# A Mamba layer with a top-2 mixture of experts: B and C of later chunks split on TensorE and ScalarE, eighteen drives by token instead of fourteen, and three steps of the routing moved

## The chip, the cores and the metric

The kernel runs on one core of a Trainium2 chip. The metric is the device time of one execution in microseconds (us), lower is better. A core has five engines with a queue each, and each works through its queue strictly in the order written: TensorE (PE, matrix products and transposes), VectorE (DVE), ScalarE (ACT), GpSimd (POOL) and SyncE (SP, which only issues DMAs). They wait for one another through semaphores.

## The reference, cut to what matters

```python
x_conv = silu(conv(x @ W_in[:, :256]));  z = x @ W_in[:, 256:]
Bm, Cm = split(x_conv @ W_x, 2)                       # 16 states each
dt = softplus(x_conv @ W_dt + b_dt)
h  = exp(dt * A_n) * h + (dt * u) * B_n               # over time, for each of 16 states n
y  = sum_n(h * C_n) + x_conv * D
x  = layernorm(x + (y * silu(z)) @ W_out)             # 2 x 1024 tokens, 128 wide
# then: top 2 of 8 experts by x @ w_g, capacity 640, gelu MLP 128 -> 512 -> 128,
# weighted sum back, residual, layernorm
```

## The kernel before, in words

The 2048 tokens are worked in four chunks (0 to 3) of 512 tokens, and each chunk in 16 units, one for each state: 64 units, numbered U = 0 to 63. U is in chunk U // 16 and has the place n = U % 16 there. The 256 channels lie as two halves d = 0, 1 of 128 partitions.

What a unit needs, and who makes it:

- **decay**, exp(dt * A_n): ScalarE, two 128x512 instructions into PSUM (`decays`, L1074).
- **drive**, dt * u * B_n. The usual way: TensorE spreads the row B_n over all partitions (`spread_b`, one matmul, L648), VectorE multiplies it with dtu (`drives`, one 128x1024 instruction, L1649), between the two scans of the unit before. The other way, for the units in the table `TURNED`: ScalarE makes it with tokens in partitions (`drive_by_token`, four 128x256 instructions, L1105, into the one buffer `drive_t`), and TensorE turns it back with two times four transposes (`turn_drive`, L664). Such a "turned" unit has no VectorE drive, and its decay is one 128x1024 instruction into `decay_sb` (L1069). The two PSUM banks of spread rows are also those of the turned drives, so the drive of the unit behind a turned one is made a unit earlier (`drive_beside`).
- **scan**: VectorE, two 128x512 scans (L1678), d = 0 and d = 1.
- **product** with C_n: GpSimd, one 128x1024 instruction (`multiply`, L1436). The states have a ring of 3 buffers, the products 4.
- **sum** into y: TensorE, `add_to_y`, eight 128x128 transposing matmuls (L678), in the last chunk four instructions of 512 columns (L673). It is queued two or more units behind (`SUMS`).

Around the units each engine's loop holds the rest of the layer, at a place n that tables or `if n ==` give: the projections of the next chunk (`bc_job`, `dt_job`, `conv_job`, `z_job` on TensorE, `take_...` and `soften_...` on ScalarE, `finish_dt` and `times_u` on GpSimd), and the end of the chunk before: `gate` on VectorE, then `start_y`, `turn_y` and `project_out` on TensorE, then the routing (`sort`, `mark`, `take_ranks`, `share`, `place_weights` on VectorE; `score`, `add_exps`, `weigh` on GpSimd) and 8 scatters of rows to the experts' slots, issued one per unit from GpSimd (`scatter`, L1517).

B and C of a chunk are kept to float32 precision as three bfloat16 parts in `bc_parts`. Chunk 0's parts are made on VectorE. For chunks 1 to 3 `take_bc` on ScalarE writes the leading part, and `split_bc` on GpSimd makes the rest with three 128x512 instructions (L1446, L1448, L1450), which two DMAs of SyncE's queue bring into place (`place_parts`).

`JOBS` lists the users of the two PSUM banks in which these side jobs pass (bank 0, 1; bank 2 for the last ranks), in order: a job waits until the one before it in its bank has been taken. `PAUSES` (units 30 and 61) are where ScalarE changes its table for silu.

Behind unit 63 come the routing of chunk 3, its scatters, and the experts: an MLP stage that TensorE fills.

## Time and profile before

| | |
|---|---|
| median of 3 runs | 385.12 us (383.41 to 385.39) |
| the profiled execution | 384.32 us, its span 382.6 us |
| busy in the span | PE 286.2 us, DVE 282.6 us, ACT 211.8 us, POOL 266.2 us |
| first scan to last | 24.91 to 255.1 us |
| first scan of chunk 1, 2, 3 | 79.51, 137.90, 196.87 us |

In rows of the timeline the columns are start, duration, engine, line, operation, output <- inputs, count and, in brackets, idle time before with the one who released it. Merged rows (x2 and more) give the time from the first's start to the last's end. DVE instructions overlap a little: a drive of 1.20 us is followed by the next instruction 1.11 to 1.12 us after its start. TensorE's rows likewise.

### The profile page before, as it was taken

How to read it: one execution, taken by the hardware profiler on the slowest of the kernel's cores; microseconds unless marked ns; L12 is line 12 of the kernel's file. 1: busy time of each engine (PE TensorE's matmuls, PEld its weight loads, DVE VectorE, ACT ScalarE, POOL GpSimd, SP SyncE). 2: the span in 40 equal slices, each digit the busy share in tenths (PEclk: the TensorE clock that was granted, in tenths of full speed). 3: DMA queues.
4: the chain of work that ended last, by engine and by line, in shares of the span. 5: the costliest groups of instructions: out<-in, count | busy, mean ns of one | idle time of the engine just before them, and what ended most of it. 6: DMA issues, size and time to landing. Idle time of an engine off the chain costs nothing. (4 is left out here: it accounts for less than half of the span.)

```text
span 382.6 us, 5173 instructions
## 1 busy us (share of the span) xinstructions
PE 286.2 (75%) x1566; PEld 207.6 (54%) x1566; DVE 282.6 (74%) x429; ACT 211.8 (55%) x425; POOL 266.2 (70%) x226
## 2 busy tenths in 40 slices
PE   8797889678866867786545899774289999998700
PEld 6445547456745544675433454332278888887600
DVE  2699889999999899999899889986021333334565
ACT  2858987969675684777737455744003323331305
POOL 4507689978888999999999876985710555556532
PEclk9999999999999868997885999899589999999965
DMA  7061079473354263232123211001152444222873
GB/s 233 6 224 55 2 240 286 135 194 127 89 168 137 82 199 117 69 100 82 55 73 122 74 64 55 3 15 42 43 155 79 118 126 125 82 82 76 240 204 110
DMA packets 35786, 42.90 MB, mean 112 GB/s; under 512 B 3862, under 2 KB 26331, under 8 KB 35760
## 3 DMA queue, kind: packets, MB, share of 16 engines
q1 hardware_dynamic: 32336, 37.38, 31.9%
q0 software_dynamic: 2304, 4.24, 3.4%
q10 hardware_dynamic: 1120, 0.97, 0.8%
q8 instruction: 12, 0.20, 0.2%
q14 instruction: 14, 0.11, 0.1%
HBM read 30.11 MB, written 12.79 MB: 112 GB/s over the span
## 5 line engine op out<-in xcount | busy, mean ns | idle before, releaser
L1436 POOL TENSOR_TENSOR product<-state,c_wide 128x1024 f32<-128x1024 f32 x64 | 149.9, 2347 | 37.1 <-DVE state L1678 27.5
L1074 ACT ACTIVATE psum<-dt,a_neg 128x512 f32<-128x512 f32 x96 | 65.0, 686 | 53.1 <-DVE state L1678 51.8
L678 PE MATMUL psum<-ident,product 128*128 128x128 f32 x384 | 56.1, 295 | 24.5 <-POOL product L1436 24.5
L678 PEld LDWEIGHTS psum<-ident,product 128*128 128x128 f32 x384 | 47.4, 152 | 35.0 <-POOL product L1436 32.1
L1678 DVE TENSOR_TENSOR_SCAN state<-psum,drive 128x512 f32<-128x512 f32 x52 | 62.0, 1212 | 2.5 <-ACT psum L1074 2.3
L1649 DVE TENSOR_TENSOR drive<-dtu,psum 128x1024 f32<-128x1024 f32 x50 | 60.0, 1199 | 4.6 <-PE psum L648 4.5
L1678 DVE TENSOR_TENSOR_SCAN state<-psum,carry,drive 128x512 f32<-128x512 f32 x48 | 60.0, 1269 | 0.2
L1563 POOL DMA_INDIRECT result_rows<-state,result_at x30 | 30.3, 1010 | 40.7 <-DVE state L1892 33.4
L1517 POOL DMA_INDIRECT slot_rows<-sent,scatter_at x32 | 32.9, 1028 | 10.7 <-issue 6.6
L912 PE MATMUL psum<-product,fc_sb 128*128 128x320 f32 x128 | 36.1, 435 | 1.1 <-DVE product L1860 1.1
L1857 DVE TENSOR_SCALAR tags<-c_wide 128x10 f32<-128x10 f32 x8 | 1.3, 164 | 43.4 <-PE psum L901 43.4
L1337 ACT ACTIVATE u<-psum 128x640 f32<-128x640 f32 x16 | 11.3, 704 | 38.6 <-PE psum L912 37.9
L673 PE MATMUL psum<-product,ident 128*128 128x512 f32 x60 | 29.4, 619 | 1.6 <-POOL product L1436 1.6
L912 PEld LDWEIGHTS psum<-product,fc_sb 128*128 128x128 f32 x128 | 22.8, 190 | 11.3 <-issue 2.7
L1337 ACT ACTIVATE z_tok<-psum 128x640 f32<-128x640 f32 x16 | 11.3, 704 | 27.6 <-PE psum L912 18.8
L664 PE MATMUL psum<-ident,drive_t 128*128 128x128 f32 x112 | 18.7, 296 | 8.6 <-DVE drive L1649 7.6
L723 PE MATMUL psum<-x_chan,w_conv 128*128 128x512 f32 x48 | 23.4, 614 | 1.6 <-ACT sent L1178 1.6
L1105 ACT ACTIVATE drive_t<-dtu_t,b_t 128x256 f32<-128x256 f32 x56 | 23.7, 494 | 1.0 <-PE psum L664 0.9
L664 PEld LDWEIGHTS psum<-ident,drive_t 128*128 128x128 f32 x112 | 14.4, 152 | 16.1 <-issue 14.3
L648 PE MATMUL psum<-bc_parts,selector 128*128 128x512 bf16 x50 | 20.0, 404 | 2.0 <-DVE state L1678 1.5
L1678 DVE TENSOR_TENSOR_SCAN state<-decay_sb,carry,psum 128x512 f32<-128x512 f32 x16 | 19.6, 1261 | 0.4 <-issue 0.4
L673 PEld LDWEIGHTS psum<-product,ident 128*128 128x128 f32 x60 | 11.5, 200 | 14.0 <-issue 10.7
(256 smaller groups left out, 527.1 us busy)
## 6 DMA issues: line engine op xcount, KB each, us to landing
c_wide<-c_rows SPq DMA_DIRECT2D x32, 512.0 KB
slot_rows<-blank SPq DMA_DIRECT2D x8, 325.0 KB, 4.6
c_wide<-slot_rows SPq DMA_DIRECT2D x8, 325.0 KB, 3.4
result_rows<-zeros SPq DMA_DIRECT2D x8, 256.0 KB, 5.1
late_rows<-zeros SPq DMA_DIRECT2D x8, 256.0 KB
fc_sb<-in_c_fc SPq DMA_DIRECT2D x8, 256.0 KB
proj_sb<-in_c_proj SPq DMA_DIRECT2D x8, 256.0 KB
c_wide<-result_rows SPq DMA_DIRECT2D x8, 256.0 KB, 5.5
```

The costliest lines, as they stand in the source:

```text
L664: last = nc.tensor.transpose(psum[:, turned_bank(U, d), j * P:(j + 1) * P], drive_t[:, j, d * P:(d + 1) * P], ident[:, :])
L673: nc.tensor.matmul(psum[:, Y_BANK + d, :], ident[:, :], product[:, i, d, :], start=False, stop=True, skip_group_check=True).then_inc(summe ...
L678: last = nc.tensor.matmul(y_part(j, d), product[:, i, d, j * P:(j + 1) * P], ident[:, :], is_transpose=True, start=False, stop=True, skip_ ...
L723: last = nc.tensor.matmul(psum[:, bank, :], w_conv[:, k, d * P:(d + 1) * P], x_of(q, k), start=(k == 0), stop=(k == D_CONV - 1))
L912: last = nc.tensor.matmul(psum[:, 2 + 2 * (h % 2) + s, 0:HALF], fc_sb[:, i, h * P:(h + 1) * P], rows_chan[:, i, s * HALF:(s + 1) * HALF], ...
L1074: nc.scalar.activation(psum[:, A_BANK + d, :], dt[:, q % 2, d, :], ACT.Exp, scale=a_neg[:, n:n + 1]).then_inc(decay_ready, 1)
L1105: nc.scalar.activation(drive_t[:, j, :], dtu_t[:, j, :], ACT.Copy, scale=b_t[:, q % 2, j, n:n + 1]).then_inc(drive_t_ready, 1)
L1436: nc.gpsimd.tensor_tensor(product[:, U % PRODUCTS, channels, :], state[:, U % RING, channels, :], wide, ALU.mult).then_inc(product_ready, 1)
L1517: gp.indirect_dma_start(out=slot_rows, out_offset=bass.IndirectOffsetOnAxis(ap=scatter_at[:, k, j:j + 1], axis=0), in_=sent[:, k, j, :], i ...
L1563: gp.indirect_dma_start(out=result_rows, out_offset=bass.IndirectOffsetOnAxis(ap=result_at[:, i, s:s + 1], axis=0), in_=rows_out[:, i, s, ...
L1649: nc.vector.tensor_tensor(drive[:, drive_number(U) % 2, :, :], dtu[:, q % 2, :, :], psum[:, b_bank(U), :].unsqueeze(1).to_broadcast([P, DT ...
L1678: nc.vector.tensor_tensor_scan(state[:, U % RING, d, :], decay, rows, before, ALU.mult, ALU.add).then_inc(scanned, 1)
```

## The change

Five things are changed together.

1. `TURNED` has 18 units instead of 14: chunk 1 has 19, 21, 23, 26, 28, 31 (was 19, 22, 26, 29), chunk 2 has 43, 45, 47 (was 43, 46), chunk 3 has 51, 53, 55, 57, 60 (was 51, 54, 57, 60). There are two buffers for them: `drive_t` and, from its last use on, `conv_rows_sb`. Turned units may now stand two apart; the second one's first half then waits for the first one's second scan.
2. For chunks 2 and 3 the middle and low parts of B and C are made by TensorE and ScalarE: `rest_job` adds minus the part just cast to the same PSUM bank (one bfloat16 matmul of 512 columns), `take_rest` casts what is left, twice. `split_bc` and `place_parts` stay for chunk 1 alone.
3. `dt_job`, `take_dt_job`, `soften_...`, `finish_dt` and `times_u` of the next chunk stand at other places n, `JOBS` has another order, and `center_w_out` with `take_w_cat` moves one unit ahead.
4. `share` (the reciprocal) moves from behind unit SHARE[q] to between the two scans of the unit after it.
5. The scatters of chunk 1's rows move from n = 14, 15 of chunk 2 and n = 0 to 5 of chunk 3 to n = 4 to 11 of chunk 3.

```diff
-TURNED = (4, 7, 10, 14, 19, 22, 26, 29, 43, 46, 51, 54, 57, 60)
+TURNED = (4, 7, 10, 14, 19, 21, 23, 26, 28, 31, 43, 45, 47, 51, 53, 55, 57, 60)
...
-        drive_t = sb("drive_t", [P, TPC, D_INNER])
+        drive_t = [sb("drive_t", [P, TPC, D_INNER]), conv_rows_sb]
...
             def turn_drive(U, d):
                 pe.wait_ge(drive_t_ready, TPC * (TURNED.index(U) + 1))
                 pe.wait_ge(drive_ready, drive_number(U) + d)
+                if d == 0 and U - 2 in TURNED:
+                    pe.wait_ge(scanned, DT * (U - 1))
...
+            def rest_job(q, part):
+                bank, _ = JOB[f"bc{q}"]
+                pe.wait_ge(minus_eye_made, 1)
+                if part == 0:
+                    pe.wait_ge(bc_cast, q - 1)
+                else:
+                    pe.wait_ge(bc_parted, q - 1)
+                rows = slice(64 * part, P)
+                nc.tensor.matmul(psum[:, W_BANKS[bank], :], minus_eye[rows, :], bc_parts[rows, q * CH:(q + 1) * CH], start=False, stop=True,
+                                 skip_group_check=True).then_inc(bc_rest_made, 1)
...
                     if n == q - 1 and q < NQ - 1:
                         bc_job(q + 1)
-                    elif n in (q, 2 * q) and q < NQ - 1:
-                        dt_job(q + 1, n // q - 1)
+                    if q < NQ - 1 and n in (q + 1, q + 2):
+                        rest_job(q + 1, n - q - 1)
+                    if q < NQ - 1 and n in (1, 3):
+                        dt_job(q + 1, n // 2)
+                    if q == 2 and n == 4:
+                        dtu_job(2, 0)
...
+            def take_rest(q, part):
+                bank, _ = JOB[f"bc{q}"]
+                act.wait_ge(bc_rest_made, 2 * (q - 2) + part + 1)
+                lanes = slice(64 + 32 * part, P)
+                nc.scalar.activation(bc_parts[lanes, q * CH:(q + 1) * CH], psum[lanes, W_BANKS[bank], :], ACT.Copy).then_inc(w_taken[bank] if part else bc_parted, 1)
...
-                    if n >= PLACE[q] and U < LAST - 1:
+                    if n >= PLACE[q] and q != 2 and U < LAST - 1:
                         scatter_some(q - 1, n - PLACE[q], 1)
-                    if q >= 2 and n < RUNS // NQ - EARLY[q - 1]:
-                        scatter_some(q - 2, n + EARLY[q - 1], 1)
+                    if q == 2 and n < RUNS // NQ - EARLY:
+                        scatter_some(0, n + EARLY, 1)
+
+                    if q == 3 and PLACE[q] - RUNS // NQ <= n < PLACE[q]:
+                        scatter_some(1, n - PLACE[q] + RUNS // NQ, 1)
...
                 scan(U, 0)
                 if drive_beside(U):
                     drives(drive_beside(U))
+                if q and n == SHARE[q] + 1:
+                    share(q - 1)
                 scan(U, 1)
...
-                    if n == SHARE[q]:
-                        share(q - 1)
```

The first place is TensorE at units 18 to 20, the start of chunk 1. L578 (L584 in the changed kernel) with `w_dt_sb` is a `dt_job`, L664 (L677) a `turn_drive`, L632 (L638) is `start_y`, L678 (L691) `add_to_y`, L648 (L658) `spread_b`. Before:

```order
L578 MATMUL psum<-u,w_dt_sb 128x512 x2
L664 MATMUL psum<-ident,drive_t 128x128 x4
L578 MATMUL psum<-u,w_dt_sb 128x512 x2
L664 MATMUL psum<-ident,drive_t 128x128 x4
L632 MATMUL psum<-diag_d,u 128x128 x8
L678 MATMUL psum<-ident,product 128x128 x16
L648 MATMUL psum<-bc_parts,selector 128x512
```

and in the changed kernel, with L727 the new `rest_job`:

```order
L584 MATMUL psum<-u,w_dt_sb 128x512 x2
L677 MATMUL psum<-ident,drive_t 128x128 x4
L727 MATMUL psum<-bc_parts,minus_eye 128x512
L677 MATMUL psum<-ident,drive_t 128x128 x4
L638 MATMUL psum<-diag_d,u 128x128 x8
L691 MATMUL psum<-ident,product 128x128 x16
L727 MATMUL psum<-bc_parts,minus_eye 128x512
L584 MATMUL psum<-u,w_dt_sb 128x512 x2
```

The second `dt_job` of the chunk has moved from ahead of the first unit's sums to behind them, together with a `rest_job`, and both stand ahead of the spread that follows.

The second place is ScalarE at units 34 to 36 of chunk 2. L1074 (L1103) are decays, L1082 (L1111) a copy of the last state, L1021 and L1022 (L1050, L1051) are the two halves of a `take_dt_job`. Before:

```order
L1117 ACTIVATE bc_sb<-psum 128x512
L1118 ACTIVATE bc_parts<-psum 128x512
L1074 ACTIVATE psum<-dt,a_neg 128x512 x2
L1082 ACTIVATE carry<-state 128x2
L1021 ACTIVATE soft<-psum,channel_sb 128x512
L1022 ACTIVATE dt<-psum,channel_sb 128x512
L1074 ACTIVATE psum<-dt,a_neg 128x512 x2
L1082 ACTIVATE carry<-state 128x2
L1021 ACTIVATE soft<-psum,channel_sb 128x512
L1022 ACTIVATE dt<-psum,channel_sb 128x512
```

and in the changed kernel, with L1157 the new `take_rest`:

```order
L1149 ACTIVATE bc_sb<-psum 128x512
L1150 ACTIVATE bc_parts<-psum 128x512
L1050 ACTIVATE soft<-psum,channel_sb 128x512
L1051 ACTIVATE dt<-psum,channel_sb 128x512
L1103 ACTIVATE psum<-dt,a_neg 128x512 x2
L1111 ACTIVATE carry<-state 128x2
L1157 ACTIVATE bc_parts<-psum 64x512
L1050 ACTIVATE soft<-psum,channel_sb 128x512
L1051 ACTIVATE dt<-psum,channel_sb 128x512
L1103 ACTIVATE psum<-dt,a_neg 128x512 x2
```

Both halves of dt are taken one unit sooner, and a `take_rest` stands ahead of the second. TensorE's queue there has its `start_y`, the sum of unit 32, the spread for unit 37, the `rest_job` and then the `dt_job` that this take waits for.

The third place is GpSimd in chunk 3, units 51 to 57, with L1436 (L1478) the product and L1517 (L1557) a scatter. Before:

```order
L1436 TENSOR_TENSOR product<-state,c_wide 128x1024
L1517 DMA slot_rows<-sent,scatter_at 5120x130
L1436 TENSOR_TENSOR product<-state,c_wide 128x1024
L1517 DMA slot_rows<-sent,scatter_at 5120x130
L1436 TENSOR_TENSOR product<-state,c_wide 128x1024
L1517 DMA slot_rows<-sent,scatter_at 5120x130
L1436 TENSOR_TENSOR product<-state,c_wide 128x1024 x4
L1477 TENSOR_SCALAR half_var<-sum_squares 128x4
```

and in the changed kernel:

```order
L1557 DMA slot_rows<-sent,scatter_at 5120x130
L1478 TENSOR_TENSOR product<-state,c_wide 128x1024
L1557 DMA slot_rows<-sent,scatter_at 5120x130
L1478 TENSOR_TENSOR product<-state,c_wide 128x1024
L1557 DMA slot_rows<-sent,scatter_at 5120x130
L1478 TENSOR_TENSOR product<-state,c_wide 128x1024
L1557 DMA slot_rows<-sent,scatter_at 5120x130
L1478 TENSOR_TENSOR product<-state,c_wide 128x1024
L1517 TENSOR_SCALAR half_var<-sum_squares 128x4
```

The scatters of the first units are gone (seven products stand together ahead of this piece), and the products of units 54 to 56, which stood together, now have a scatter between them. The same holds for units 57 to 59: `score`, `add_exps` and `weigh` each have a scatter behind them in the changed kernel.

## Rows read from the trace of the kernel before

**Rows 1.** The page's head.

```profile
span 382.6 us, 5173 instructions
```

**Rows 2.** Busy by stretch: start:end, length, PE, PEld, DVE, ACT, POOL, PE clock, DMA, GB/s.

```profile
198.00:255.00 57.00, 44.87 (x152) 24.15 (x152) 54.17 (x70) 35.46 (x70) 48.36 (x38) 0.85 0.17 57
...
150.40:153.80 3.40, 3.40 (x18) 3.40 (x17) 3.40 (x4) 1.62 (x4) 2.93 (x3) 0.50 0.26 84
```

**Rows 3.** The page's groups: busy, mean ns of one, idle before and its releaser.

```profile
L1436 POOL TENSOR_TENSOR product<-state,c_wide 128x1024 f32<-128x1024 f32 x64 | 149.9, 2347 | 37.1 <-DVE state L1678 27.5
L1074 ACT ACTIVATE psum<-dt,a_neg 128x512 f32<-128x512 f32 x96 | 65.0, 686 | 53.1 <-DVE state L1678 51.8
...
L1649 DVE TENSOR_TENSOR drive<-dtu,psum 128x1024 f32<-128x1024 f32 x50 | 60.0, 1199 | 4.6 <-PE psum L648 4.5
...
L1105 ACT ACTIVATE drive_t<-dtu_t,b_t 128x256 f32<-128x256 f32 x56 | 23.7, 494 | 1.0 <-PE psum L664 0.9
```

**Rows 4.** ScalarE's groups: a decay in one piece.

```profile
L1069 ACT ACTIVATE decay_sb<-dt,a_neg 128x1024 f32<-128x1024 f32 x14 | 15.9, 1136 | 0.0
```

**Rows 5.** VectorE's timeline: gate and drive in chunk 1, reciprocals, last weights.

```profile
89.95 1.19 DVE L1685 TENSOR_TENSOR z_tok<-z_tok,psum 128x1024 f32<-128x1024 f32 x1
...
95.58 1.22 DVE L1649 TENSOR_TENSOR drive<-dtu,psum 128x1024 f32<-128x1024 f32 x1 [0.89 <-PE psum L648]
...
128.26 0.18 DVE L1766 RECIPROCAL denom<-denom 128x4 f32<-128x4 f32 x1 [1.23 <-POOL denom L1497]
...
190.84 0.18 DVE L1766 RECIPROCAL denom<-denom 128x4 f32<-128x4 f32 x1 [1.58 <-POOL denom L1497]
...
245.26 0.17 DVE L1808 TENSOR_TENSOR sent<-weight,psum 128x8 f32<-128x8 f32 x1
```

**Rows 6.** TensorE's timeline behind the gate of chunk 1.

```profile
91.63 1.95 PE L632 MATMUL psum<-diag_d,u 128*128 128x128 f32 x16
93.41 1.91 PE L678 MATMUL psum<-ident,product 128*128 128x128 f32 x16
95.16 0.38 PE L648 MATMUL psum<-bc_parts,selector 128*128 128x512 bf16 x1
```

**Rows 7.** TensorE's timeline, chunk 3: output projection to a turned drive.

```profile
218.50 0.70 PE L770 MATMUL psum<-w_cat,y_chan 128*128 128x136 f32 x4 [1.23 <-ACT y_chan L1169]
...
219.96 0.60 PE L664 MATMUL psum<-ident,drive_t 128*128 128x128 f32 x4
```

**Rows 8.** TensorE's timeline behind the gate of chunk 2.

```profile
149.52 3.00 PE L632 MATMUL psum<-diag_d,u 128*128 128x128 f32 x16 [2.40 <-DVE z_tok L1685]
...
153.92 0.38 PE L648 MATMUL psum<-bc_parts,selector 128*128 128x512 bf16 x1
...
155.23 1.88 PE L578 MATMUL psum<-u,w_dt_sb 128*128 128x512 f32 x4
```

**Rows 9.** VectorE's timeline, second scan of unit 36.

```profile
155.48 1.22 DVE L1678 TENSOR_TENSOR_SCAN state<-psum,drive 128x512 f32<-128x512 f32 x1
```

**Rows 10.** GpSimd's timeline: a scatter; units 42, 46's weights; units 52, 55, 56, 57; weights.

```profile
144.53 1.01 POOL L1517 DMA_INDIRECT slot_rows<-sent,scatter_at  x1 [0.17 <-issue]
...
178.20 2.35 POOL L1436 TENSOR_TENSOR product<-state,c_wide 128x1024 f32<-128x1024 f32 x1 [0.93 <-issue]
...
193.07 0.21 POOL L1501 TENSOR_TENSOR weight<-exps,denom 128x8 f32<-128x8 f32 x1
...
215.78 2.36 POOL L1436 TENSOR_TENSOR product<-state,c_wide 128x1024 f32<-128x1024 f32 x1 [0.79 <-DVE state L1678]
...
226.47 2.37 POOL L1436 TENSOR_TENSOR product<-state,c_wide 128x1024 f32<-128x1024 f32 x1 [1.20 <-PE psum L673]
231.16 2.37 POOL L1436 TENSOR_TENSOR product<-state,c_wide 128x1024 f32<-128x1024 f32 x1 [2.32 <-DVE state L1678]
234.64 2.36 POOL L1436 TENSOR_TENSOR product<-state,c_wide 128x1024 f32<-128x1024 f32 x1 [1.11 <-issue]
...
245.02 0.20 POOL L1501 TENSOR_TENSOR weight<-exps,denom 128x8 f32<-128x8 f32 x1
```

More of the change, by code:

```diff
@@ L475, in _ @@
                     store_c(m // (D_STATE // C_PAIR) + 1)
-                if m % (D_STATE // C_PAIR) == 6 and m // (D_STATE // C_PAIR) < NQ - 1:
-                    place_parts(m // (D_STATE // C_PAIR) + 1)
+                if m == 6:
+                    place_parts(1)
                 if m == C_SLOTS - 1:
@@ L637, in spread_b @@
                 if n == 0 and q:
-                    pe.wait_ge(bc_taken, 32 * q)
+                    if q == 1:
+                        pe.wait_ge(bc_taken, 32)
+                    else:
+                        bank, before = JOB[f"bc{q}"]
+                        pe.wait_ge(w_taken[bank], before + 1)
                 if U >= 2:
@@ L847, in _ @@
                     turn_drive(U + 1, 0)
-                if q == 2 and n in (6, 7):
-                    dtu_job(2, n - 6)
+                if q == 2 and n == 7:
+                    dtu_job(2, 1)
                 if q == 2 and n in (12, 14):
@@ L1095, in drive_by_token @@
                 q, n = divmod(U, D_STATE)
-                before = TURNED.index(U)
-                act.wait_ge(drive_turned, DT * before)
+                i = TURNED.index(U)
+                if i == 1:
+                    act.wait_ge(w_conv_made, 1)
+                if i >= 2:
+                    act.wait_ge(drive_turned, DT * (i - 1))
                 act.wait_ge(b_t_ready, q + 1)
@@ L1250, in _ @@
                         drive_by_token(T)
-                if q == 2 and n in (6, 7):
-                    take_dtu(2, n - 6)
+                if q == 2 and n in (4, 7):
+                    take_dtu(2, n // 7)
                 if q == 2 and n in (13, 15):
@@ L1267, in _ @@
                         take_bc(q + 1)
-                    elif n == first + 1:
+                    if q and n in (first + 1, first + 2):
+                        take_rest(q + 1, n - first - 1)
+                    if n == (first + 1, 2, 2)[q]:
                         take_dt_job(q + 1, 0)
-                    elif n == first + 2:
+                    elif n == (first + 2, 3, 3)[q]:
                         take_dt_job(q + 1, 1)
-                    elif n == first + 3:
+                    elif n == (first + 3, 4, 5)[q]:
                         soften_exp(q + 1)
-                    elif n == (first + 4 if q == 0 else first + 5):
+                    elif n == first + (5 if q == 2 else 4):
                         soften_log(q + 1)
@@ L1297, in _ @@
                         take_dtu(1, n - 14)
+                    if n == 15:
+                        take_w_cat()
                 else:
@@ L1318, in _ @@
                         copy_sent(q - 1)
-                    if q == 1 and n == 0:
-                        take_w_cat()
                     if q == NQ - 1 and n == 10:
@@ L1523, in scatter_some @@
                     scatter(i // TPC, TPC * q + i % TPC)
-            EARLY = [D_STATE - n for n in PLACE]
+            EARLY = D_STATE - PLACE[1]
             U_PLACE = (NQ - 1) * D_STATE + PLACE[NQ - 1]
```

39 lines of the change are left out of this document (22 added, 17 removed).

## The prediction

> **What bounds the kernel now.** I read the page's head and busy shares first, then busy time by stretch, then VectorE's timeline through all 64 units, and beside it those of GpSimd, TensorE and ScalarE wherever VectorE stood idle. The profiled execution took 384.3 us around a span of 382.6 [rows 1]; the median of the runs shown is 385.1, 0.8 above it. VectorE sets the pace of the units: in chunk 3 it is busy 54.2 of 57.0 us [rows 2], and a unit costs it two scans of about 1.2 and a drive of 1.2 [rows 3]. But GpSimd is close behind: 48.4 of the same 57.0 us, and the reader should see that its slack is not spread evenly. In chunk 2, from the product of unit 42 at 178.20 to the weights at 193.07, it works without a break [rows 10], and the reciprocal that waits 1.58 us is waiting for it [rows 5]. TensorE and ScalarE have time in sum, but their queues are in order, and a side job ahead of a spread or a decay delays VectorE.
>
> **Part 1, the four drives.** Each drive that leaves VectorE saves 1.12 us, since the next instruction starts that long after a drive of 1.20 [rows 3]. Two leave in chunk 1, one in chunk 2, one in chunk 3: 4.5 us. ScalarE takes four 128x256 instructions for each, 23.7 / 14 = 1.7 us [rows 3], and gives back two decays of 0.69 for one of 1.14 [rows 3, 4]: 1.5 us net, 6 us in all, into 53.1 us of its waiting for scans [rows 3]. As a sum that is hidden; place by place it is not, below.
>
> **Part 2, the split.** It frees GpSimd of three instructions in chunks 1 and 2, early in the chunk, where it waits for scans anyway: by itself nothing. On TensorE the two matmuls of a chunk cost like a spread, 0.4 us each [rows 6].
>
> **Part 3, what the moved jobs do in chunk 1.** The spread that unit 20's drive waits for starts at 95.16, behind `start_y` and two sums, and VectorE already idles 0.89 us there [rows 5, 6]. Now a rest matmul and a dt job stand between: next start 0.2 and 1.8 later, as the job's four matmuls take 1.88 [rows 8]. The same dt job leaves the place ahead of `start_y`, which can begin at the gate's end, 91.1 instead of 91.63 [rows 5, 6]: 0.4 back. So the drive comes 1.6 us late (bounds 0 and 2.3: full cover, and no 0.4 back). ScalarE takes that dt (two instructions of about 0.7) only from 97.0 on, and has queued behind it a drive by token (1.7), a softplus step, two decays, the whole decay of unit 23, a softplus step and two copies of y, about 1.0, 1.3, 1.1, 1.0 and 1.0, with pieces of 128x1024 at up to 1.14 [rows 3, 4]: y is copied at about 105.1. The output projection waits for it and stands ahead of the second half of turned unit 23. From such a projection's start to the end of the transposes was 219.96 + 0.60 - 218.50 = 2.1 us in chunk 3 [rows 7], and here 0.4 of B's transposes come on top: 107.6. VectorE would want it at 97.2 + 1.1 (drive) + 1.2 (scan) + 2.4 (unit 21) + 3.5 (unit 22) + 1.2 = 106.5. Cost 1.1 (0 to 2). At unit 23 the run is 1.6 + 1.1 late and one drive ahead, 1.6 behind before.
>
> The rest of chunk 1 pays: a second drive (1.1), and the reciprocal. It waited 1.23 us [rows 5] for sums that stood behind GpSimd's `times_u`; that is two units earlier now, and the reciprocal 2.3 later. The weights need GpSimd's next product to end, which leaves about 1.1 of the 1.23. Chunk 1: +1.6 - 1.1 - 1.1 = -0.6.
>
> **Chunk 2.** ScalarE must have the decay of unit 37 ready when unit 36's second scan ends, 155.48 + 1.12 = 156.6 [rows 9]. Its queue now holds, ahead of that decay, the take of a dt job that TensorE starts behind the spread of 153.92 and a rest matmul, at 154.35, and ends at 156.2 [rows 8]. Take 1.25, decay 0.65: 158.05. VectorE waits 1.4 us (0 to 1.5). TensorE is late partly because its granted clock was 0.50, the 1.2 GHz level, from 150.4 to 153.8 [rows 2]: `start_y` took 3.00 where it took 1.95 in chunk 1 [rows 6, 8]. I take the stretch as it was.
>
> The extra turned unit, 47, saves 1.1. The reciprocal saves nothing here. GpSimd's chain from the product of unit 42 to the weights is the same 193.07 - 178.20 = 14.9 us [rows 10]: five products, `times_u`, `score` and `add_exps`, none of them moved against unit 42. `place_weights` stands on VectorE behind the second scan of unit 46 and ends where it did. The 1.58 us just pass from the reciprocal to the weights. Chunk 2: +1.4 - 1.1 = +0.3.
>
> **Chunk 3.** The two scatters at the end of chunk 2 and six at the start of chunk 3 go to where VectorE is to become fastest. A scatter holds GpSimd 1.01 + 0.17, with the next start 1.2 later [rows 10]. Ahead of the weights that `place_weights` needs, counted from the product of unit 52, there were two scatters and there are now seven: 5 x 1.23 = 6.1 us. GpSimd's idle time there was 1.20 + 2.32 + 1.11 = 4.6 [rows 10]; it fills that, less about 0.3 in which it still waits for unit 57. So the weights come 6.1 - 4.6 + 0.3 = 1.8 later, and with them VectorE, which wrote them at 245.26 [rows 5], at once behind GpSimd's 245.02 [rows 10]. The fifth turned unit of the chunk saves VectorE 1.1, which it waits away at the weights. Chunk 3: +1.8 (bounds -2.3, if GpSimd keeps up and two TensorE waits between units 54 and 55 also go, and +3). Behind unit 63 the queues are the same, and the experts simply start as much later.
>
> **The sum:** -0.6 + 0.3 + 1.8 = +1.5, from the execution's own 384.3: 385.8. In the terms of the median 0.8 is added, 386.6; I give 386.2, between the two. A measurement of this kernel tells about 0.5%, 1.9 us, from no change, so my forecast reads as no difference, on the slow side.
>
> The trace shows TensorE at the lower level behind the gate of chunk 2 after it had been idle 2.4 us [rows 8]. The Trainium skill (TensorE: Matmul & The Clock Gate, section "What's actually happening") says the clock follows how busy TensorE has lately been, and the change gives it more work. By that rule the 1.4 us of chunk 2 would go. It would be 384.8 instead of 386.2; the trace agrees with the rule in that the level fell after idling.
>
> **Rivals.**
>
> - *VectorE alone bounds, and all cover holds.* 4.5 saved by drives and 1.23 + 1.58 by reciprocals [rows 5]: 7.3 off, 377.0 to 377.8. For it speaks VectorE's 95% in chunk 3 [rows 2]; against it GpSimd's unbroken 14.9 us, which no edit shortens.
> - *GpSimd keeps up in chunk 3.* If the weights don't wait, chunk 3 gives -2.3 instead of +1.8: 382.1. For it: GpSimd idles 4.6 us there and starts the chunk free of lag. Against it: 6.1 is more than 4.6.
> - *TensorE at its lower level behind the gate of chunk 1* (the slower side). There `start_y`, sums, spread, dt job, transposes and the projection now follow one another on the path. Sized by `start_y`, 3.00 against 1.95, a factor of 1.5 on 1.8 + 1.8 + 2.0 + 2.5 = 8 us: +4.1, and 390.3. It decides once the level falls between 91 and 106. For it: it fell behind chunk 2's gate [rows 2]. Against it: chunk 1's `start_y` ran fast [rows 6], and TensorE has more to do there now.
> - *TensorE at its full level behind the gate of chunk 2*: `start_y` 1.05 and the sum faster, so that the dt is taken in time; -1.4, and 384.8.
>
> **How the numbers follow.** Forecast 0.46; all cover holds 0.08; GpSimd keeps up 0.17; lower level in chunk 1 0.13; full level in chunk 2 0.16. The forecast's own range is 384.4 to 388.2, by its bounds of about 1 us each way on three terms. With no more than 2 in 10 left out, the range reaches down past the second rival and most of the way to the third: 381.6 to 389.4. Faster by over 0.5% means under 383.2: the first two rivals and a little of the others, 0.28. Slower by over 0.5% means above 387.1: the third rival and a third of the forecast's cases, 0.29. Within 0.5%: 0.43.
>
> **What would show it.** In the changed profile: VectorE's drive for unit 22 (its first behind unit 19) waits 2 to 3 us for a spread, not 0.89; the second scan of unit 23 waits about 1 us; the first scan of unit 37 waits over 1 us for a decay on ScalarE; the reciprocal waits under 0.3 us in chunk 1, and in chunk 2 the write of weights waits about 1.2; in chunk 3 GpSimd shows no gap from unit 52's product to the weights except about 0.3, and VectorE waits over 2 us in reciprocal and weights together. The forecast is wrong if the scatters hold GpSimd under 1 us each, if the weights are ready when VectorE comes to them, or if the drives' gains are still there at the first scan of chunk 2 and again at that of chunk 3.

## The result, and the profile after

The changed kernel takes 388.53 us in the median (386.78 to 389.56, 6 runs); the kernel before, on the same chip, 385.19 (383.41 to 385.44, 6 runs). The ratio is 1.0101 with an interval of 1.0077 to 1.0125: slower by 3 to 5 us. The prediction said 386.2 within 381.6 to 389.4. The time lies in the range, but 2.3 us above the figure and just above the 384.4 to 388.2 that the forecast allowed its own case. "No difference, on the slow side" had 0.43 of the chances and "slower by over 0.5%" 0.29; it is the second that was measured.

The page of the changed kernel, its head and two groups (busy us, mean ns | idle before and its releaser):

```profile
span 386.8 us, 5258 instructions
...
L1721 DVE TENSOR_TENSOR_SCAN state<-psum,drive 128x512 f32<-128x512 f32 x50 | 59.7, 1213 | 4.9 <-ACT psum L1103 4.7
L1692 DVE TENSOR_TENSOR drive<-dtu,psum 128x1024 f32<-128x1024 f32 x46 | 55.2, 1201 | 8.3 <-PE psum L658 8.2
```

VectorE does 46 drives, 55.2 us, where it did 50 in 60.0 [rows 3]. But the idle time in front of them rose from 4.6 to 8.3 us, behind TensorE's spreads, and that in front of this group of scans, behind ScalarE's decays, from 2.5 to 4.9. So the work was removed as planned, and the wait took its place.

The same in time. The columns are the stretch, its length, busy us and instructions of each engine, TensorE's granted clock and the DMAs. Each stretch goes from the first scan of a chunk to that of the next, the last one from the last scan to the end. First the kernel before:

```profile
79.51:137.90 58.39, 43.04 (x263) 31.38 (x262) 55.96 (x73) 42.25 (x82) 49.42 (x36) 0.96 0.44 139
137.90:196.87 58.97, 41.37 (x253) 32.60 (x251) 56.50 (x75) 39.78 (x88) 55.11 (x42) 0.87 0.29 95
196.87:255.05 58.18, 45.21 (x155) 24.15 (x152) 55.35 (x71) 36.42 (x72) 49.50 (x39) 0.85 0.17 57
255.05:382.60 127.55, 91.10 (x579) 76.20 (x579) 50.60 (x152) 34.78 (x78) 59.58 (x58) 0.88 0.38 111
```

and the changed kernel:

```profile
79.48:140.02 60.54, 45.76 (x272) 33.34 (x270) 53.81 (x71) 45.27 (x89) 45.61 (x32) 0.94 0.44 128
140.02:198.48 58.46, 41.82 (x253) 33.53 (x254) 55.51 (x74) 43.44 (x95) 52.34 (x39) 0.85 0.32 99
198.48:259.43 60.95, 46.80 (x171) 24.56 (x169) 54.26 (x70) 37.06 (x74) 49.48 (x39) 0.89 0.17 56
259.43:386.80 127.37, 90.82 (x579) 75.77 (x579) 51.56 (x151) 34.75 (x78) 60.31 (x58) 0.88 0.39 111
```

Chunk 1 is 2.15 us longer (60.54 against 58.39), chunk 2 0.51 shorter, chunk 3 2.77 longer, the experts 0.18 shorter: 4.2 us in the span. VectorE's busy time fell by 2.15, 0.99 and 1.09 us, which is what was bought.

Its waits, from VectorE's timeline of the changed kernel (start, duration, what it is, idle time before it and the releaser):

```profile
99.67 1.22 DVE L1692 TENSOR_TENSOR drive<-dtu,psum 128x1024 f32<-128x1024 f32 x1 [5.00 <-PE psum L658]
110.35 1.28 DVE L1721 TENSOR_TENSOR_SCAN state<-decay_sb,carry,psum 128x512 f32<-128x512 f32 x1 [1.26 <-issue]
...
144.18 1.22 DVE L1721 TENSOR_TENSOR_SCAN state<-psum,drive 128x512 f32<-128x512 f32 x1 [0.72 <-ACT psum L1103]
...
159.17 1.22 DVE L1721 TENSOR_TENSOR_SCAN state<-psum,drive 128x512 f32<-128x512 f32 x1 [0.31 <-ACT psum L1103]
184.89 1.22 DVE L1721 TENSOR_TENSOR_SCAN state<-psum,drive 128x512 f32<-128x512 f32 x1 [0.88 <-ACT psum L1103]
192.38 1.22 DVE L1721 TENSOR_TENSOR_SCAN state<-psum,drive 128x512 f32<-128x512 f32 x1 [0.68 <-ACT psum L1103]
...
215.74 1.22 DVE L1692 TENSOR_TENSOR drive<-dtu,psum 128x1024 f32<-128x1024 f32 x1 [2.09 <-PE psum L658]
245.67 0.18 DVE L1809 RECIPROCAL denom<-denom 128x4 f32<-128x4 f32 x1 [0.76 <-POOL denom L1537]
249.83 0.17 DVE L1851 TENSOR_TENSOR sent<-weight,psum 128x8 f32<-128x8 f32 x1 [2.70 <-POOL weight L1541]
```

The first row answers to the drive that waited 0.89 us [rows 5]: it now waits 5.00. The reciprocals of chunks 1 and 2, which waited 1.23 and 1.58, wait no more; that of chunk 3 and the write of weights wait 3.5 us together, where the write came at once behind GpSimd. The second row, 1.26 us, is the second scan of unit 23.

Behind the first row stands TensorE, in the changed kernel, from ahead of the gate to the spread:

```profile
85.92 0.60 PE L677 MATMUL psum<-ident,drive_t 128*128 128x128 f32 x4
89.43 0.58 PE L727 MATMUL psum<-bc_parts,minus_eye 128*128 128x512 bf16 x1 [2.91 <-ACT bc_parts L1150]
...
91.18 3.78 PE L638 MATMUL psum<-diag_d,u 128*128 128x128 f32 x16 [0.30 <-DVE z_tok L1728]
94.75 2.44 PE L691 MATMUL psum<-ident,product 128*128 128x128 f32 x16
97.12 0.39 PE L727 MATMUL psum<-bc_parts,minus_eye 64*128 64x512 bf16 x1
97.44 1.98 PE L584 MATMUL psum<-u,w_dt_sb 128*128 128x512 f32 x4
99.26 0.38 PE L658 MATMUL psum<-bc_parts,selector 128*128 128x512 bf16 x1
```

In the kernel before, two dt jobs stood there, with a shorter idle time ahead of each:

```profile
85.82 1.98 PE L578 MATMUL psum<-u,w_dt_sb 128*128 128x512 f32 x4 [1.71 <-ACT w_cat L1229]
...
89.37 1.98 PE L578 MATMUL psum<-u,w_dt_sb 128*128 128x512 f32 x4 [1.13 <-ACT bc_parts L1118]
```

TensorE's granted clock there (the column behind the bracket), in the changed kernel:

```profile
88.00:90.00 2.00, 0.57 (x2) 0.75 0.00 0
90.00:92.00 2.00, 1.70 (x9) 0.50 0.92 258
...
96.00:98.00 2.00, 2.00 (x14) 1.00 0.48 127
```

and in the kernel before:

```profile
90.00:92.00 2.00, 2.00 (x12) 1.00 0.90 262
```

`start_y` took 3.78 where it took 1.95, and the sums 2.44 where they took 1.91 [rows 6]: the clock was at its 1.2 GHz level (0.50), and back at the full one by 96 us. Of the 4.1 us that the wait grew, 1.83 + 0.53 is clock, less the 0.45 by which `start_y` began sooner, and 0.32 + 1.82 are the rest matmul and the dt job ahead of the spread (next start minus start).

In chunk 3 it is GpSimd, here from unit 52 to the weights:

```profile
218.29 2.34 POOL L1478 TENSOR_TENSOR product<-state,c_wide 128x1024 f32<-128x1024 f32 x1 [3.33 <-DVE state L1721]
...
236.20 2.36 POOL L1478 TENSOR_TENSOR product<-state,c_wide 128x1024 f32<-128x1024 f32 x1
...
241.44 1.09 POOL L1557 DMA_INDIRECT slot_rows<-sent,scatter_at  x1 [0.32 <-DVE state L1721]
...
246.23 1.04 POOL L1557 DMA_INDIRECT slot_rows<-sent,scatter_at  x1 [0.59 <-PE psum L686]
...
249.60 0.20 POOL L1541 TENSOR_TENSOR weight<-exps,denom 128x8 f32<-128x8 f32 x1
```

From the product of unit 52 to that of 57 no gap is left: five times product and scatter, (236.20 - 218.29) / 5 = 3.6 us each, while VectorE needs 3.5 for a unit with a drive and 2.4 for a turned one. From unit 52's product to the weights it takes 249.60 - 218.29 = 31.3 us, where it took 245.02 - 215.78 = 29.2 [rows 10].

The other part of chunk 3 lies ahead of unit 52: its product starts 218.29 - 198.48 = 19.8 us after the chunk's first scan, and it was 215.78 - 196.87 = 18.9. VectorE waited 2.09 us for the spread there where it had waited 1.17. This is the clock again. `start_y` has another form in this chunk, four matmuls; before and after:

```profile
210.32 2.64 PE L625 MATMUL psum<-u,diag_d 128*128 128x512 f32 x4
```
```profile
211.93 3.56 PE L631 MATMUL psum<-u,diag_d 128*128 128x512 f32 x4
```

It took 0.92 us longer, and the wait behind it is 0.92 longer. The gate was passed at the lower level in both kernels, but in the kernel before the granted clock was 1.00 from 212 us, and in the changed one still 0.50 up to 214 and 0.68 up to 216.

### The profile page after: what moved, and what is told of

It reads as the page before. It is cut to its first block and busy times, and to the rows that moved or that the text cites. A ratio compares the mean times of both kernels' runs of the same rounds, so it can differ in the third digit from the quotient of the medians.

```text
span 386.8 us, 5258 instructions
## 1 busy us (share of the span) xinstructions
PE 291.2 (75%) x1598; PEld 211.0 (55%) x1598; DVE 279.3 (72%) x425; ACT 219.1 (57%) x441; POOL 260.5 (67%) x221
## 5 line engine op out<-in xcount | busy, mean ns | idle before, releaser
L1478 POOL TENSOR_TENSOR product<-state,c_wide 128x1024 f32<-128x1024 f32 x64 | 149.9, 2347 | 47.4 <-DVE state L1721 38.9
L1103 ACT ACTIVATE psum<-dt,a_neg 128x512 f32<-128x512 f32 x88 | 59.0, 684 | 34.4 <-DVE state L1721 33.2
L691 PE MATMUL psum<-ident,product 128*128 128x128 f32 x384 | 54.1, 288 | 14.2 <-POOL product L1478 13.9
L1721 DVE TENSOR_TENSOR_SCAN state<-psum,drive 128x512 f32<-128x512 f32 x50 | 59.7, 1213 | 4.9 <-ACT psum L1103 4.7
L1692 DVE TENSOR_TENSOR drive<-dtu,psum 128x1024 f32<-128x1024 f32 x46 | 55.2, 1201 | 8.3 <-PE psum L658 8.2
L691 PEld LDWEIGHTS psum<-ident,product 128*128 128x128 f32 x384 | 46.2, 149 | 24.2 <-POOL product L1478 20.1
L1721 DVE TENSOR_TENSOR_SCAN state<-psum,carry,drive 128x512 f32<-128x512 f32 x42 | 52.8, 1271 | 0.4 <-ACT psum L1103 0.2
L1557 POOL DMA_INDIRECT slot_rows<-sent,scatter_at x32 | 32.8, 1025 | 10.4 <-issue 6.5
L1721 DVE TENSOR_TENSOR_SCAN state<-decay_sb,carry,psum 128x512 f32<-128x512 f32 x22 | 27.1, 1263 | 2.1 <-issue 1.7
L1098 ACT ACTIVATE decay_sb<-dt,a_neg 128x1024 f32<-128x1024 f32 x18 | 20.5, 1139 | 7.7 <-DVE state L1721 7.7
L658 PE MATMUL psum<-bc_parts,selector 128*128 128x512 bf16 x46 | 17.7, 389 | 3.7 <-DVE state L1721 2.9
L1721 DVE TENSOR_TENSOR_SCAN state<-decay_sb,psum 128x512 f32<-128x512 f32 x14 | 16.5, 1204 | 1.0 <-issue 1.0
L677 PE MATMUL psum<-ident,conv_rows_sb 128*128 128x128 f32 x72 | 11.5, 284 | 7.3 <-ACT drive_t L1137 2.8
```

The source lines that it names most:

```text
L691: last = nc.tensor.matmul(y_part(j, d), product[:, i, d, j * P:(j + 1) * P], ident[:, :], is_transpose=True, start=False, stop=True, skip_ ...
L1103: nc.scalar.activation(psum[:, A_BANK + d, :], dt[:, q % 2, d, :], ACT.Exp, scale=a_neg[:, n:n + 1]).then_inc(decay_ready, 1)
L1478: nc.gpsimd.tensor_tensor(product[:, U % PRODUCTS, channels, :], state[:, U % RING, channels, :], wide, ALU.mult).then_inc(product_ready, 1)
L1557: gp.indirect_dma_start(out=slot_rows, out_offset=bass.IndirectOffsetOnAxis(ap=scatter_at[:, k, j:j + 1], axis=0), in_=sent[:, k, j, :], i ...
L1692: nc.vector.tensor_tensor(drive[:, drive_number(U) % 2, :, :], dtu[:, q % 2, :, :], psum[:, b_bank(U), :].unsqueeze(1).to_broadcast([P, DT ...
L1721: nc.vector.tensor_tensor_scan(state[:, U % RING, d, :], decay, rows, before, ALU.mult, ALU.add).then_inc(scanned, 1)
```

## The experiments

My theory after this reading: four separate things happened. Scatters late in chunk 3 hold GpSimd; a dt job stands ahead of the spread behind chunk 1's gate; an idle TensorE lets the clock fall there; and what the drives and the reciprocal give is taken in part by GpSimd's chain. The rival is that the turned units overload ScalarE and the rest is noise around them. In the table medians are in us; the last column has the lengths of the chunks in us, from VectorE's timeline of one profiled execution each, cut at the first scan of each chunk as above (before 58.4, 59.0, 58.2; changed kernel 60.5, 58.5, 61.0). A chunk's length can differ by 1 us between two executions of the same instructions: up to unit 45 f2 has those of the kernel before, and its chunk 2 is already 0.9 us longer by then (59.9 in all, for 59.0). Line numbers in the rows below are those of the kernel they are from.

| kernel | median | before, same chip | ratio [interval] | chunk 1, 2, 3 |
|---|---|---|---|---|
| e1 turned alone | 384.21 | 385.85 | 0.9963 [0.9947, 0.9979] | 57.7, 59.9, 57.4 |
| e2 reciprocal alone | 385.56 | 385.85 | 0.9999 [0.9981, 1.0017] | 58.4, 59.0, 58.3 |
| e3 old scatters | 384.93 | 385.85 | 0.9985 [0.9969, 1.0002] | 60.6, 58.5, 57.6 |
| e4 split alone | 392.91 | 385.85 | 1.0157 [1.0121, 1.0193] | 63.1, 58.9, 59.1 |
| f1 fill idle | 384.29 | 385.30 | 0.9969 [0.9946, 0.9992] | 58.3, 58.5, 58.1 |
| f2 late scatters alone | 388.10 | 385.30 | 1.0063 [1.0043, 1.0083] | 58.5, 59.9, 61.6 |
| f3 weights later | 383.13 | 385.30 | 0.9938 [0.9907, 0.9968] | 56.6, 61.3, 58.1 |
| f4 dt behind spread | 385.07 | 385.30 | 0.9988 [0.9958, 1.0018] | 59.7, 58.4, 58.1 |
| g1 both orders | 383.41 | 385.62 | 0.9952 [0.9933, 0.9971] | 57.7, 58.3, 57.5 |
| g2 sixteen turned | 382.59 | 385.62 | 0.9935 [0.9910, 0.9960] | 57.7, 57.7, 57.4 |
| g3 weights of chunk 2 later | 383.90 | 385.62 | 0.9962 [0.9944, 0.9980] | 58.5, 58.6, 59.1 |
| h1 both and sixteen | 385.52 | 385.34 | 1.0005 [0.9987, 1.0023] | 60.2, 59.3, 58.3 |

**e1, the turned units alone.**

```diff
-TURNED = (4, 7, 10, 14, 19, 22, 26, 29, 43, 46, 51, 54, 57, 60)
+TURNED = (4, 7, 10, 14, 19, 21, 23, 26, 28, 31, 43, 45, 47, 51, 53, 55, 57, 60)
+drive_t in two buffers, with the waits that go with them
```

> The kernel before with one part of the change alone: the eighteen turned units (and the second buffer that they need). B and C are still split on GpSimd, no job is moved. My theory: the drives themselves are worth about 1.1 us each, 4 x 1.1 = 4.5 us less, so about 380.7 where before has 385.2; the loss of the whole change comes from the jobs and scatters that were moved. Rival: ScalarE's queue has no room, decays come late in chunks 1 and 2 as they do after the change, and half or more of it is given back: 383 to 385.

1.4 us less (0.37%), not 4.5: a third of what four drives are worth. VectorE's timeline of this kernel says who took the rest:

```profile
126.97 0.18 DVE L1771 RECIPROCAL denom<-denom 128x4 f32<-128x4 f32 x1 [2.34 <-POOL denom L1502]
140.79 1.22 DVE L1683 TENSOR_TENSOR_SCAN state<-psum,drive 128x512 f32<-128x512 f32 x1 [0.80 <-ACT psum L1076]
```

In chunk 1 one of the two drives went into the reciprocal, 2.34 us for 1.23 [rows 5]. In chunk 2 two decays of ScalarE came late (0.80 where 0.19 was waited before, and 0.89), and another 0.7 us of waits stands at 164 to 166; the chunk became 0.9 us longer. So the rival is right for chunk 2, GpSimd's chain for chunk 1.

**e2, the reciprocal alone.**

```diff
                     drives(drive_beside(U))
+                if q and n == SHARE[q] + 1:
+                    share(q - 1)
                 scan(U, 1)
...
-                    if n == SHARE[q]:
-                        share(q - 1)
```

> The kernel before with only the reciprocal moved behind the first scan of the next unit. My theory: its wait of 1.23 us in chunk 1 goes (1.1 kept), the 1.58 us of chunk 2 pass on to the write of weights: 1.1 less, 384.1 where before has 385.2. Rival: both waits go, 2.8 less, 382.4. Another rival: the write of weights takes over the wait in both chunks, no change, 385.2.

Nothing, with an interval of 0.7 us each way: the last rival. In chunk 1 the reciprocal has no wait left, and the write of weights has it:

```profile
130.64 0.17 DVE L1808 TENSOR_TENSOR sent<-weight,psum 128x8 f32<-128x8 f32 x1 [1.00 <-POOL weight L1501]
```

**e3, the old scatters in the changed kernel.**

```diff
-                    if n >= PLACE[q] and q != 2 and U < LAST - 1:
+                    if n >= PLACE[q] and U < LAST - 1:
...
-                    if q == 3 and PLACE[q] - RUNS // NQ <= n < PLACE[q]:
-                        scatter_some(1, n - PLACE[q] + RUNS // NQ, 1)
+                    if q >= 2 and n < RUNS // NQ - EARLY[q - 1]:
+                        scatter_some(q - 2, n + EARLY[q - 1], 1)
```

> The changed kernel with the scatters of chunk 1 back in their old places (two at the end of chunk 2, six at the start of chunk 3). My theory: five scatters fewer stand ahead of the weights in chunk 3, the 2.7 us wait of VectorE there goes: 2 to 2.8 us less, about 386.1 where the changed kernel has 388.5. Rival: the scatters then delay the products at the start of chunk 3 and give the same back: within 0.5 us of 388.5.

The ratio to before goes from 1.0101 to 0.9985: without the late scatters the change as a whole gains and loses nothing that can be measured. Chunk 3 is 57.6 us instead of 61.0, 3.4 less, more than I had from the wait at the weights alone (2.70), since the reciprocal's 0.76 goes too.

**e4, the split alone**: the changed kernel with these taken back, so that the split stays, with its job table and moved jobs.

```diff
-TURNED = (4, 7, 10, 14, 19, 21, 23, 26, 28, 31, 43, 45, 47, 51, 53, 55, 57, 60)
+TURNED = (4, 7, 10, 14, 19, 22, 26, 29, 43, 46, 51, 54, 57, 60)
-                if q and n == SHARE[q] + 1:
-                    share(q - 1)
+                    if n == SHARE[q]:
+                        share(q - 1)
+and the scatters as in e3
```

> The kernel before with the split of B and C by TensorE and ScalarE alone, and with it the dt jobs and the other jobs that it moves; turned units, reciprocal and scatters as before. My theory: TensorE is late with the spread behind the gate of chunk 1 (3 to 5 us wait instead of 0.9) and ScalarE with decays in chunks 1 and 2: 3 to 5 us more, about 389 where before has 385.2. Rival: the split only frees GpSimd and its jobs hide, within 1 us of 385.2; then the turned units are what overloads ScalarE.

The dearest part by its ratio: 1.6%, some 6 us, though its six executions spread from 389.3 to 394.6. Its first drive behind the gate waits 5.04 us, as after the whole change, and 4.7 of the 5.6 us that its last scan ends late lie in chunk 1. The profiled execution is the slowest of the six, and 4.5 us of its excess lie behind the last scan (132.0 us for 127.6), where the granted clock was 0.67 from 290.7 to 300.7 and the kernel before had 1.00 as far behind its last scan. Only the part up to the last scan is traced to the edit; how much of the 6 us the rest makes in the other executions stays open.

**f1, TensorE's idle time filled** (on e3).

```diff
+                    if q == 1 and n == 2:
+                        dt_job(2, 0)
                     if q < NQ - 1 and n in (q + 1, q + 2):
                         rest_job(q + 1, n - q - 1)
-                    if q < NQ - 1 and n in (1, 3):
+                    if q < NQ - 1 and n in (1, 3) and (q, n) != (1, 1):
                         dt_job(q + 1, n // 2)
```

> The changed kernel with the old places of the scatters, and with the first dt job of chunk 1 one unit later, ahead of the first rest matmul, where TensorE stood idle 2.9 us before its granted clock fell to 0.50. Its output is taken no sooner than it was, so nothing on the path moves. Theory of the clock: the level falls because of the idle time; with 1.0 us of it left the level stays at 1.00 from 90 to 96 us, `start_y` takes 1.95 and the two sums 1.9 (3.78 and 2.44 in the changed kernel), and the wait of VectorE's first drive behind the gate falls from 5.0 to about 2.6 us: 383 where the kernel with old scatters has 384.9. Rival, the order alone: the level falls all the same or makes no difference, and the wait stays at 5 us; 384.9.

The wait fell to 2.77 us, chunk 1 by 2.2 us. On TensorE, and its clock from 90 to 91 us:

```profile
89.79 0.38 PE L727 MATMUL psum<-bc_parts,minus_eye 128*128 128x512 bf16 x1 [1.55 <-ACT bc_parts L1152]
...
91.53 2.05 PE L638 MATMUL psum<-diag_d,u 128*128 128x128 f32 x16 [0.92 <-DVE z_tok L1727]
93.42 1.91 PE L691 MATMUL psum<-ident,product 128*128 128x128 f32 x16
```
```profile
90.00:91.00 1.00, 0.61 (x5) 1.00 0.54 193
```

The dt job is the same work on the same engine, 2 us later, and the level did not fall. This is one execution; the four that were profiled with the 2.91 us of idle time (changed kernel, e3, e4, f4) all had `start_y` at 3.78 or 3.79. 2.77 is near what the prediction's own sum gives (0.89 + 1.6 = 2.5). The whole time gained less, 384.3 for 384.9, and the intervals of the two ratios overlap: waits of 2.24 (for 2.10) and 0.8 us came in chunk 3, which is 0.6 us longer.

**f2, the late scatters alone** (on the kernel before, the lines of e3 the other way round).

> The kernel before with only the scatters of chunk 1 moved to just ahead of the weights of chunk 3. Theory of the prediction: GpSimd has 4.6 us idle there against 6.1 us of scatters, so 1.5 to 1.8 us more: 387.3 where before has 385.6. Theory of the first runs: the five scatters cost their full 3.4 us, as between the changed kernel and the one with old scatters: 389. Rival: nothing below 0.5 us, since VectorE is slower here than in the changed kernel and GpSimd keeps up: 385.6.

2.8 us more, between the two theories; chunk 3 alone is 3.4 us longer (61.6 for 58.2), 0.4 of it at the gate's spread (1.60 for 1.17), which leaves 2.9, in waits of 1.65 at the reciprocal and 1.54 at the weights. The prediction had 1.8 for it. The gaps that I took as filled are not: GpSimd still idles 1.04 us ahead of unit 56's product at 232.24, and 0.31 and 0.59 ahead of the scatters behind `score` and `add_exps`, 1.9 us and not 0.3.

**f3, the weights a unit later** (on the kernel before, with eighteen turned units and the reciprocal moved).

```diff
-        PLACE = [0, 13, 14, 12]
+        PLACE = [0, 14, 15, 12]
```

> The kernel before with the eighteen turned units, the reciprocal moved, and the write of weights and all that waits for it one unit later in chunks 1 and 2. Theory: GpSimd's chain up to the weights took in the drives' gains (VectorE's wait at the reciprocal rose to 2.34 and 1.72 us with the turned units alone); one unit later it is hidden, and both waits fall under 0.3: 3 to 4 us less than the turned units alone, 380.5 to 381.5 where before has 385.6. Rival: GpSimd is the bound over the whole chunk, the wait comes back at another place, and the time stays near 384.

383.1, and not 381: GpSimd's waits went, chunk 1 is the shortest of all (56.6), and then ScalarE is late. VectorE's timeline:

```profile
126.38 1.28 DVE L1683 TENSOR_TENSOR_SCAN state<-psum,carry,drive 128x512 f32<-128x512 f32 x1 [1.33 <-ACT psum L1076]
141.29 1.22 DVE L1683 TENSOR_TENSOR_SCAN state<-psum,drive 128x512 f32<-128x512 f32 x1 [2.00 <-ACT psum L1076]
```

ScalarE's queue shows why. It had stood 4.46 us for GpSimd's `score`, with decays behind that wait; and the far decays share a bank with the ranks, so they waited for the write of weights:

```profile
124.39 0.21 ACT L1214 ACTIVATE exps<-above 128x12 f32<-128x12 f32 x1 [4.46 <-POOL above L1494]
...
133.69 1.30 ACT L1064 ACTIVATE psum<-dt,a_neg 128x512 f32<-128x512 f32 x2 [1.28 <-DVE sent L1813]
```

**f4, the dt job behind the spread** (on e3).

```diff
+                if U == D_STATE + 4:
+                    dt_job(2, 1)
                 if q and n < 2:
                     add_to_y(U - 2)
...
-                    if q < NQ - 1 and n in (1, 3):
+                    if q < NQ - 1 and n in (1, 3) and (q, n) != (1, 3):
...
-                    elif n == (first + 2, 3, 3)[q]:
+                    elif n == (first + 2, 4, 3)[q]:
...
-                    elif n == (first + 3, 4, 5)[q]:
+                    if n == (first + 3, 4, 5)[q]:
```

> The changed kernel with the old places of the scatters, and with the second dt job of chunk 1 behind the spread that VectorE's first drive after the gate waits for, instead of ahead of it. Theory of the order: the spread comes 1.8 us sooner, the wait falls from 5.0 to 3.2 us, and what the job itself delays later is hidden: 1.5 us less, 383.4 where the kernel with old scatters has 384.9. Rival: ScalarE's queue then brings y and the projection later, the second scan of unit 23 waits that much longer, and the time stays at 384.9.

The wait fell by 2.0 us, where 1.8 was expected, to 3.05 (clock still 0.50 from 90 to 94 us), and 0.67 + 0.23 came back at the next scans. The time is 385.07 for e3's 384.93: no gain that can be measured, as the rival had it.

**g1, the edits of f1 and f4 together** (on e3).

> The changed kernel with the old places of the scatters and with both moves of the last runs: the first dt job fills TensorE's idle time ahead of the gate, the second stands behind the spread. Theory: clock (2.2 us of the 5.0 us wait) and order (1.8 us) are separate causes and add up: the wait falls to about 1 us, as in the kernel before, and the time to 382.5 to 383 where the kernel with old scatters alone has 384.9. Rival: the 1.8 us of the order come back at the second half of unit 23 and at decays, as half of them did with the second move alone: 384, like the first move alone.

The two add up: VectorE's drive behind the gate

```profile
95.92 1.22 DVE L1693 TENSOR_TENSOR drive<-dtu,psum 128x1024 f32<-128x1024 f32 x1 [0.96 <-PE psum L658]
```

waits 0.96 us, as in the kernel before, and the time is 383.4, 0.5% under before. The second half of unit 23 still waits 1.27, though the dt job no longer stands ahead of the spread. ScalarE's queue says why:

```profile
101.89 1.15 ACT L1102 ACTIVATE decay_sb<-dt,a_neg 128x1024 f32<-128x1024 f32 x1 [0.54 <-DVE state L1722]
102.95 1.04 ACT L1182 ACTIVATE soft<-soft 128x1024 f32<-128x1024 f32 x1
103.89 1.07 ACT L1212 ACTIVATE y_chan<-psum 128x512 f32<-128x512 f32 x2
```

It has 0.54 us to spare ahead of unit 23's decay; behind that, a softplus step of 1.04 us stands ahead of the copy of y that the projection waits for. In e1, where that step stands behind the copy, the same scan waits 0.32.

**g2, sixteen turned units on the kernel before**, the reciprocal moved, and in chunk 2 the weights a unit later.

```diff
+TURNED = (4, 7, 10, 14, 19, 21, 23, 26, 29, 43, 46, 51, 53, 55, 57, 60)
-        PLACE = [0, 13, 14, 12]
+        PLACE = [0, 13, 15, 12]
```

> The kernel before with sixteen turned units (21 and 23 for 22, 53 and 55 for 54; 29 stays, and chunk 2 keeps 43 and 46), the reciprocal moved, and the write of weights one unit later in chunk 2 alone. Theory: of the eighteen, those that meet ScalarE with decays queued (28 and 31, 47) pay nothing; the other two pay 1.1 us each, less what GpSimd's chain takes of it in chunk 1, and the later write saves 1.6 in chunk 2: 382 where before has 385.3 and the turned units alone 384.2. Rival: the wait at the weights of chunk 1 takes that chunk's drive, and chunk 2's gain goes into ScalarE's decays: 384.

382.6, the lowest median: 0.65% under the kernel before and about 1.6% under the changed one, by the two ratios. It can't be told from f3 (0.9935 and 0.9938). It needs neither the split nor a moved dt job.

**g3, only the reciprocal moved, and chunk 2's weights a unit later** (g2 without its TURNED).

> The kernel before with its fourteen turned units, the reciprocal moved, and the write of weights one unit later in chunk 2. Theory: VectorE waits there for GpSimd's chain alone, 1.58 us at the reciprocal, 0.47 and 1.07 us at reciprocal and weights once the reciprocal is moved; a unit later both are hidden: 1.5 us less, 383.8 where before has 385.3. Rival: the wait passes on again, to a decay of ScalarE or to the gate of chunk 3: 385.3.

383.9, 0.4% less than before, as the median was expected. The profile doesn't carry the reason cleanly: chunk 2 is only 0.4 us shorter and chunk 3 0.9 longer (2.25 us at its gate for 1.17, behind a `start_y` of 3.62 for 2.64, the clock once more). In chunk 2 VectorE waits 1.1 us from 166 to 171, as f2 does (0.20, 0.21, 0.66), and the profiled execution of the kernel before does not. So what the median gained is not located.

**h1, both orders of g1 with the TURNED and PLACE of g2.**

> The changed kernel with the old places of the scatters, both moves of TensorE's jobs, sixteen turned units in place of eighteen (29 for 28 and 31, none for 47), and the write of weights of chunk 2 one unit later. Theory: the four waits of ScalarE's decays (0.7, 0.3, 0.9, 0.7 us) come from the drives by token that stand ahead of them at the end of chunk 1 and in chunk 2; with two fewer they go, 2.6 us, against 2.2 us for two drives that VectorE does itself again: 382.5 to 383 where both moves alone give 383.4 and the kernel before with sixteen turned units 382.6. Rival: what remains of the split frees GpSimd where it was late, and the two gains add: 381 or less.

A miss by 2.5 to 3 us, and the most instructive one. The decays came as the theory had it: of the waits of 0.7, 0.3, 0.9 and 0.7 us the first is down to 0.19 and the last two are gone. The second rose. TensorE's instructions up to chunk 1's spread are those of g1, with the same idle times of 1.55 and 0.91 us. In g1 `start_y` took 2.05 us; in h1, on TensorE and then on VectorE:

```profile
90.47 3.38 PE L638 MATMUL psum<-diag_d,u 128*128 128x128 f32 x16 [0.91 <-DVE z_tok L1729]
...
150.63 3.17 PE L638 MATMUL psum<-diag_d,u 128*128 128x128 f32 x16 [2.60 <-DVE z_tok L1729]
```
```profile
96.28 1.22 DVE L1693 TENSOR_TENSOR drive<-dtu,psum 128x1024 f32<-128x1024 f32 x1 [2.29 <-remote]
...
159.27 1.22 DVE L1722 TENSOR_TENSOR_SCAN state<-psum,drive 128x512 f32<-128x512 f32 x1 [1.46 <-ACT psum L1107]
```

The level had fallen at both gates. And with it fallen at the second, unit 37 waits 1.46 us for its decay: the 1.4 that the prediction charged there, and that the changed kernel, with `start_y` at 2.05, did not pay (0.31). These are single executions, h1's 1.4 us above its median and g1's 1.0 below; that the lower level also makes the miss of the median is not shown.

## Why the prediction was right, and where it wasn't

- **Drives, 1.1 us each: right as a size, shown as busy time** (4.2 us less VectorE in three chunks). That they stay was true only where no other engine's chain ends there; e1 kept 1.4 of 4.5.
- **Chunk 1, the spread: +1.6 forecast, +4.1 found.** The order was sized right (f4: 2.0 back). What the forecast left to a rival with a chance of 0.13, the lower clock level behind this gate, came: 2.4 us by the rows, 2.2 when f1 took it away. It was sized as a factor of 1.5 over 8 us; it was a factor of 1.9 on `start_y` (3.78 for 1.95), and over by 96 us. The step that failed is "TensorE has more to do there now", which was held against it. TensorE had more to do, but a dt job had left the place ahead of the gate and a wait for ScalarE's `bc_cast` had come: 2.91 us idle at one piece where there had been 1.71 and 1.13.
- **Chunk 1, unit 23: +1.1 forecast, 1.26 found.** In the changed kernel the queue of ScalarE runs as it was followed, 2.5 us later throughout. But the reason given, the dt taken late, is not what the wait hangs on: with the dt job out of the way it is still 1.27 (f4, g1), by the softplus step that stands ahead of the copy of y.
- **The reciprocal in chunk 1: -1.1 forecast and found in the changed kernel, by one of the two reasons given at most.** e2 shows that moving it pays nothing; the wait passes to the weights. In the changed kernel neither waits, with less work for GpSimd ahead (the split gone, and `times_u` two units sooner, as the forecast had it) and VectorE itself late by then; no run takes these apart.
- **Chunk 2: +0.3 forecast, -0.5 found.** The decay of unit 37 cost 0.31 and not 1.4, since the fourth rival held there (`start_y` 2.05); h1 shows the forecast's price when the level falls. The chain of GpSimd from unit 42 to the weights is as long as I said, and the reciprocal's 1.58 us did not become a gain: they turned into two late decays, 0.88 + 0.68, and a third, 0.72 for 0.19, came at the start of the chunk.
- **Chunk 3: +1.8 forecast, +2.8 found.** From unit 52 to the weights it was 2.1, near the 1.8 (GpSimd's idle time left there was 0.32 + 0.59 us, where I had 0.3). The missing step is that this chain starts at unit 52, and unit 52 came 0.9 later than chunk 3 itself, by a spread that waited 2.09 us and not 1.17, since the lower clock level lasted further into `start_y` (3.56 for 2.64). I had such waits only as something that could go.
- **The chances.** The slow side was right, its size short. That the time lies in the range is in part luck: the sum's error of 2.7 us is made of +2.7, -0.8 and +1.0 by chunk, two of which offset each other, and of the three forecasts by chunk only that of chunk 3 had the right sign. The two largest terms that were missing, 2.2 for the clock in chunk 1 and 0.9 at the gate of chunk 3, came on top of the forecast's mechanisms and not in their place. Both are the clock. I had made it an alternative, with a price and a chance of its own: 1.5 + 2.2 + 0.9, less 1.1 for unit 37, is 3.5, near the 4.2 us of the span and the 3.3 of the medians.

## What to carry to other kernels

Work taken from the engine that sets the pace pays only up to the nearest chain on another engine: look for the last wait of each stage, and move the consumer of that chain (here the write of weights, one unit later, 0.4% by itself in g3) before or with the work. Of an edit that moves side jobs in an in-order queue, ask for each place that it empties as well as for each that it fills: here the emptied place ahead of a gate cost as much as the filled one behind it. Rivals that rest on different engines are not alternatives; they add, and the range should hold their sum.
